# Stacking queries and keys by transfers inside the SBUF instead of by 0/1 matmuls, in a gated cross-attention and mixture-of-experts block

## The reference, cut to what matters

```python
# x (16, 256, 256), ctx (16, 256, 256): 16 batches, 256 tokens, 256 features; 16 heads of 16 dims
q = proj(layernorm(x), w_q, b_q); k = proj(ctx, w_k, b_k); v = proj(ctx, w_v, b_v)
scores = einsum('bhqd,bhkd->bhqk', q, k) / sqrt(16)
x = x + tanh(g_xattn) * (softmax(scores) @ v heads joined @ w_o.T + b_o)
# then: 8 experts of 256 -> 1024 -> 256, each token goes to its two best by sigmoid confidence * wealth
x = x + tanh(g_ffn) * sum over the two of weight * down(silu(gate(y)) * up(y)),  y = layernorm(x)
```

## Time and profile before

| | |
|---|---|
| median of 3 runs | 1134.77 us (1130.64 to 1135.57) |
| span of the profiled execution | 1132.2 us |
| TensorE busy | 1064.4 us, 94% of the span |
| VectorE, ScalarE, GpSimd busy | 57%, 48%, 33% |
| attention stage | up to about 445 us |
| one batch of the loop | 24.87 us |

### The profile page before, as it was taken

How to read it: one execution, slowest core, us unless ns; L and a number is a source line. 1 busy time by engine, 2 the same in 40 slices (tenths; PEclk the granted TensorE clock), 3 DMA queues, 4 the chain that set the end, 5 groups by cost and what they waited for, 6 DMA issues and landing times.

```text
span 1132.2 us, 24433 instructions
## 1 busy us (share of the span) xinstructions
PE 1064.4 (94%) x8310; PEld 889.4 (79%) x8310; DVE 650.5 (57%) x1577; ACT 547.2 (48%) x877; POOL 370.9 (33%) x444
## 2 busy tenths in 40 slices
PE   5799999999999978799999999999999999999994
PEld 4566677777777755475999999999679999999993
DVE  3657777877777764357444444444754444454442
ACT  4467777777777744346323333333643332333331
POOL 1223555555545542513212212212322121221221
PEclk8899999999999999999999999999999999999997
DMA  8010111111111173466312112112561121211211
GB/s 243 26 30 21 41 41 52 54 39 39 48 39 39 52 272 147 145 250 204 88 19 38 34 24 38 31 26 38 166 233 25 33 38 19 38 34 24 39 27 23
DMA packets 48698, 79.69 MB, mean 70 GB/s; under 512 B 6416, under 2 KB 42512, under 8 KB 44816
## 3 DMA queue, kind: packets, MB, share of 16 engines
q0 software_dynamic: 18080, 50.93, 16.7%
q1 hardware_dynamic: 30576, 28.23, 8.6%
HBM read 53.69 MB, written 25.18 MB: 70 GB/s over the span
## 4 chain that ended last, share of the span: by engine, by line
PE 82%; ACT 6%; DVE 3%; issue 3%; POOL 3%; DMA 2%; SPq 1%; POOLq 0%; ACTq 0%; DVEq 0%
PE up L1456 16%; PE gate L1456 16%; PE down L1468 10%; PE down L1470 5%; PE pv L583 4%; PE scores L572 4%; PE scores L533 3%; PE misc L479 3%; PE maxps L547 2%; PE gate L1502 2%; PE down L1521 2%; PE up L1502 2%; PE misc L506 2%; PE misc L515 2%; ACT probs L764 2%
## 5 line engine op out<-in xcount | busy, mean ns | idle before, releaser
L1853 POOL DMA_INDIRECT out<-y,token x64 | 101.2, 1581 | 450.3 <-DVE y L1724 351.7
L1617 ACT ACTIVATE silu<-gate 128x512 f32<-128x512 f32 x128 | 76.7, 600 | 277.3 <-PE up L1456 277.3
L1715 DVE TENSOR_TENSOR h<-silu,up 128x512 f32<-128x512 f32 x128 | 88.0, 688 | 179.4 <-ACT silu L1617 179.4
L977 DVE TENSOR_REDUCE max_neg<-maxps 128x4 f32<-128x1024 f32 x128 | 156.5, 1222 | 58.7 <-PE maxps L547 58.7
L1468 PE MATMUL down<-w_split,h_hi 128*128 128x512 f32 x512 | 185.8, 398 | 0.0
L1456 PE MATMUL gate<-x_hi,w_split 128*128 128x256 f32 x1024 | 184.4, 282 | 0.0
L1456 PE MATMUL up<-x_hi,w_split 128*128 128x256 f32 x1024 | 183.7, 281 | 0.0
L764 ACT ACTIVATE probs<-scores 128x1024 f32<-128x1024 f32 x124 | 127.3, 1027 | 78.7 <-PE scores L572 77.7
L1456 PEld LDWEIGHTS gate<-x_hi,w_split 128*128 128x128 f32 x1024 | 148.8, 188 | 3.0
L1456 PEld LDWEIGHTS up<-x_hi,w_split 128*128 128x128 f32 x1024 | 147.9, 188 | 0.0
L1470 PE MATMUL down<-w_split,h_lo 128*128 128x256 f32 x512 | 144.1, 282 | 0.0
(11 more groups left out here) (206 smaller groups left out, 1799.2 us busy)
## 6 DMA issues: line engine op xcount, KB each, us to landing
xg<-dispatched SPq DMA_DIRECT2D x40, 272.0 KB, 2.9
stage<-gate_T POOLq DMA_DIRECT2D x10, 1024.0 KB, 7.7
stage<-up_T POOLq DMA_DIRECT2D x10, 1024.0 KB, 9.8
stage<-down_T POOLq DMA_DIRECT2D x10, 1024.0 KB, 11.8
ctxT<-ctxT SPq DMA_DIRECT2D x17, 256.0 KB, 2.9
x_all<-x SPq DMA_DIRECT2D x16, 256.0 KB, 5.2
out<-x_all SPq DMA_DIRECT2D x16, 256.0 KB, 2.1
out<-y,token POOLq DMA_INDIRECT x70, 3.8
```

The source lines that it names most:

```text
L977: V.tensor_reduce(to, maxps[:], AX.X, ALU.max, negate=True).then_inc(s["max_taken"], 1)
L1617: nc.scalar.activation(silu[pair % 2][:], gate[pair % 2][:], ACT.Silu).then_inc(s_silu, 1)
L1715: V.tensor_tensor(h[pair % 2][:], silu[pair % 2][:], up[pair % 2][:], ALU.mult).then_inc(s_made, 1)
L1853: pool.indirect_dma_start(out, bass.IndirectOffsetOnAxis(token[:, t:t + 1], axis=0), y[:, t, :], None, compute_op=ALU.add).then_inc(s_adde ...
```

## The change

Batches 0 and 1 are stacked by matmuls as before. From batch 2 on SyncE stacks: after the last unit of scores of batch b is written it issues three transfers from the split keys of batch b+2 to every fourth partition of `keys`, and three for the queries. For that the three terms of a dimension lie on neighbouring partitions (`STEP` = 4 rows a dimension, three of them terms, the fourth zero or SHIFT, which is now the last row of each half), and the columns of the projections are ordered so that a transfer's source runs over all 128 partitions and its destination over 32. `max_scores` contracts over 63 rows instead of 48. The 0/1 matrices take whole 128-row blocks (twice the data to load and to convert) and live in `ctx_high` and `ctx_rest` until these are needed. In ScalarE's body `read_q` moves ahead of `exps(b, 6)`. `split` now waits for the transfers of the batch before instead of a unit.

```diff
-        UNITS = ["S0", "S1", "S2", "S3", "S4", "K0", "S5", "S6", "S7", "K1", "Q0", "Q1"]
+        UNITS = [f"S{pair}" for pair in range(HPAIRS)]
+        FIRST_PAIRS = [*range(0, HPAIRS, HC), *range(1, HPAIRS, HC)]
+        STACKED = 16 * TERMS
...
-            load(((probs[0][:, :, 0, :], pick_rows),), "picks_loaded")
+            load(((probs[0][:], pick_rows),), "picks_loaded")
...
+            def stack(b, what, to):
+                sp.wait_ge(s["q_split" if what == "Q" else "k_split"], b + 1)
+                parts = (high, rest, high) if what == "Q" else (high, high, rest)
+                for term, part in enumerate(parts):
+                    sp.dma_start(to[term::STEP].bitcast(fp32), part[what][:].bitcast(fp32)).then_inc(
+                        s["q_stacked" if what == "Q" else "k_stacked"], 16)
...
                 if back:
                     store_residual(b - 1, use)
+                if ahead:
+                    sp.wait_ge(s["unit_written"], unit(b, f"S{HPAIRS - 1}") + 1)
+                    stack(b + 2, "K", k[par])
+                    stack(b + 2, "Q", q[par])
                 if nxt:
                     store_shift(b + 1, 1 - par, use)
...
-                for i in range(QT):
-                    for part, source in (("high", high), ("rest", rest)):
-                        for half in range(HPP):
-                            r = slice(half * STACK, (half + 1) * STACK)
-                            last = mm(scores[:, half * QT + i, :], picks[f"{what} {part}"][r, i, :], source[what][r, c, :],
-                                      start=part == "high", stop=part == "rest")
+                for i in range(BLOCKS):
+                    for m, source in enumerate((high, rest)):
+                        picks = picks_of(what)[m]
+                        last = mm(scores[:, i, :], picks[:, i * P:(i + 1) * P], source[what][:, c, :], start=m == 0, stop=m == 1)
...
+                elif nth == 0:
+                    pe.wait_ge(s["k_stacked"], b * STACKED - STACKED)
+                    pe.wait_ge(s["q_stacked"], b * STACKED - STACKED)
...
-                stack_ahead("K0")
                 weigh(b, par, 1)
...
-                stack_ahead("K1")
...
-                stack_ahead("Q0")
                 weigh(b, par, 3)
-                stack_ahead("Q1")
...
                 read_pv(b, 1)
-                exps(b, 6)
                 if ahead:
                     read_q(b + 2, use)
+                exps(b, 6)
                 exps(b, 7)
...
-            def split(b, what, use, units):
+            def split(b, what, use):
                 use.read(alone, what)
-                if not is_first(b):
-                    alone.wait_ge(s["unit_written"], units)
+                if isinstance(b, int) and b == 2:
+                    alone.wait_ge(s["unit_written"], 2 * len(STACKS))
+                else:
+                    alone.wait_ge(s["q_stacked" if what == "Q" else "k_stacked"], b * STACKED - 2 * STACKED)
```

More of the change, by code:

```diff
@@ L154, in attention_stage @@
         rest = {what: sb(f"{what}_rest", [P, HC, SEQ], f32r) for what in "QK"}
-        picks = {what: sb(f"picks_{what}", [P, QT, P], f32r) for what in ("Q high", "Q rest", "K high", "K rest")}
         q = [sb(f"queries{i}", [P, HPAIRS, SEQ], f32r) for i in range(2)]
@@ L275, in read, with picks_of @@
                 eng.wait_ge(misc_read[n], uses + 1)
-        UNITS = ["S0", "S1", "S2", "S3", "S4", "K0", "S5", "S6", "S7", "K1", "Q0", "Q1"]
+        def picks_of(what):
+            held = (c_high[0], c_high[1]) if what == "Q" else (c_rest[0], c_rest[1])
+            return [part[:].rearrange("p c s -> p (c s)") for part in held]
+        UNITS = [f"S{pair}" for pair in range(HPAIRS)]
         STACKS = ["K0", "Q0", "K1", "Q1"]
+        FIRST_PAIRS = [*range(0, HPAIRS, HC), *range(1, HPAIRS, HC)]
+        STACKED = 16 * TERMS
         def units_before(b):
-            last = isinstance(b, int) and b == BATCHES - 1
-            return b * len(UNITS) + (2 * len(STACKS) if not last else len(STACKS))
+            return b * len(UNITS) + 2 * len(STACKS)
         def unit(b, what):
-            order = [n for n in UNITS if n not in STACKS] if isinstance(b, int) and b >= BATCHES - 2 else UNITS
-            return units_before(b) + order.index(what)
+            return units_before(b) + UNITS.index(what)
         def is_last(b):
@@ L860, in body @@
             def body(b, par, use, ahead, nxt, back, late):
-                def stack_ahead(what):
-                    if ahead:
-                        read_stack(par, what[0], int(what[1]), unit(b, what))
                 exps(b, 0)
@@ L971, in read_v, with maxima @@
                 last.then_inc(use.freed("V"), 1)
-            def maxima(b, pair):
-                dve.wait_ge(s["max_scored"], b * HPAIRS + (pair + 1))
+            def maxima(b, nth, order=range(HPAIRS)):
+                pair = order[nth]
+                dve.wait_ge(s["max_scored"], b * HPAIRS + (nth + 1))
                 to = max_neg[:].rearrange("p t (u n) -> p u t n", u=HPP)[:, :, :, pair]
@@ L1065, in vector_attention @@
             for n, what in enumerate("QK"):
-                for m, part in enumerate(("high", "rest")):
-                    last = V.tensor_copy(picks[f"{what} {part}"][:], probs[0][:, 2 * n + m, 0, :].rearrange("p (i c) -> p i c", i=QT))
+                for m in range(2):
+                    last = V.tensor_copy(picks_of(what)[m], probs[0][:, 2 * n + m].rearrange("p t s -> p (t s)"))
             last.then_inc(s["picks_ready"], 1)
@@ L1080, in vector_attention @@
             for pair in range(3):
-                maxima(0, pair)
+                maxima(0, pair, FIRST_PAIRS)
             rest_part(1, "K")
@@ L1086, in vector_attention @@
             read_v(0, PRO1)
-            maxima(0, 3)
-            maxima(0, 4)
+            maxima(0, 3, FIRST_PAIRS)
+            maxima(0, 4, FIRST_PAIRS)
             rest_part(1, "Q")
             for pair in range(5, HPAIRS):
-                maxima(0, pair)
+                maxima(0, pair, FIRST_PAIRS)
                 if pair < 7:
@@ L1232, in body @@
                     scale_x(b + 2)
-                    split(b + 2, "K", use, units_before(b) + (UNITS.index("K1") + 1 - len(UNITS)))
+                    split(b + 2, "K", use)
                 if isinstance(b, int) and b == 1:
@@ L1238, in body @@
                 if ahead:
-                    split(b + 2, "Q", use, units_before(b) + (UNITS.index("Q1") + 1 - len(UNITS)))
+                    split(b + 2, "Q", use)
                 if late:
@@ L1256, in gpsimd_attention @@
             return scatter_next_to_last, scatter_last
-        handed = dict(over=attention_over, s=s, units=units_before(BATCHES - 1) + sum(n not in STACKS for n in UNITS))
+        handed = dict(over=attention_over, s=s, units=units_before(BATCHES - 1) + len(UNITS))
         return sync_attention, tensor_attention, scalar_attention, vector_attention, gpsimd_attention, handed
```

49 lines of the change are left out of this document (22 added, 27 removed).

## The result

The changed kernel takes 1174.44 us (median of four runs, 1173.02 to 1177.57) against 1134.9 on the same chip: ratio 1.0343, 95% interval 1.0315 to 1.0371. It is slower, as forecast, but by 3.4% where 1.7% was forecast. The profiled execution has this span, against the 1132.2 of the earlier trace rows.

What follows compares the result with a forecast made beforehand. Bound: the loop from score 0 through the maxima's turn to the shift's landing. Thirteen steps of +0.7 and +0.55 make +16, with start and first two batches +19: span 1151, median 1154 us; forecast case 1143 to 1170, 8-in-10 range 1130 to 1192.

Steps and rivals of the forecast that it cites:

- the copy of Q: ScalarE's read_q ahead of exponentials 6: score 7 starts 0.78 us later, the turn of the maxima 0.8 later.
- The rule on which it rested: Loop from score 0 to the shift: even with free transfers a batch stays at 24.87 us, by -0.2 to +0.3.
- slow copies: Rival: SBUF-to-SBUF stacking transfers at half rate, 187 to 215 GB/s, +2.8 to +3.9 us a batch, 1174 to 1211; chance 0.2.
- not held up: Rival: stacking transfers finish before the shift's and the clock holds, -0.2 to +0.3 us a batch, 1134 to 1142; chance 0.18.
- faster: Rival: before the turn, removing K0 gains its full 0.7 us; -0.9 a batch, 1126 in total; chance 0.12.
- The thirteen steps: Score 0 to next score 0, batches 1 to 14: each +0.7 us of wait and +0.55 of clock, together +16.
- a middle: Shift's bytes, queued behind the six transfers, move between 271.35 and 273.0; 272.1 taken, score 0 at 272.9, +0.7 us a batch.
- one batch in three: TensorE idle before score 0: the clock dips in one batch in three, 1.7 us each, +0.55 a batch.
- the upper end: Clock term's range of 0 to 1.7 us a batch: at its top every batch pays for the dip.
- K0 and K1: Stacking matmuls removed before the turn: K0 gains 0 to 0.1 us, K1 nothing before the turn.
- The start: Before score 0 of batch 0: larger 0/1 matrices, longer conversions and more stacking units, 2 to 5 us, +4 taken.
- The next two steps: Batches 0 and 1 have more between turn and score 0 and lose less: -1 us against the rule.

Runs made afterwards that it cites:

- e1: Changed kernel without its six stacking transfers a batch, so later batches compute other values; 1138.5 us, ratio 1.0036.
- e9: Changed kernel with GpSimd's four scatters issued behind the context split and the bias addition; 1139.3 us, ratio 1.0030.
- e4: Changed kernel with 20 needless matmuls between the projection of V and score 0 of each batch from 2 on; 1158.4 us, ratio 1.0193.
- e15: e14 with GpSimd's addition of the bias moved from behind the context split to before the split of Q; 1151.5 us, ratio 1.0127.
- e13: Kernel before the change with only the copy of Q (read_q) moved ahead of exponentials 6; 1143.9 us, ratio 1.0067.
- e14: e11 with VectorE's statistics of the batch after next moved behind the first reduce of the maxima; 1148.5 us, ratio 1.0108.
- e18: Changed kernel, copy of Q put back, GpSimd's context split and bias ahead of Q's split, scatters held until the shift has landed; 1154.6 us, ratio 1.0168.
- e2: Changed kernel with the same six transfers at a quarter of the bytes each, so it computes other values; 1139.7 us, ratio 1.0021.
- e11: Changed kernel with the scatters late and the copy of Q put back behind exponentials 6; 1148.7 us, ratio 1.0108.
- e10: Changed kernel with the shift issued from ScalarE's queue and the next context's load held until the residual is stored; 1162.7 us, ratio 1.0223.
- e19: As e18, but with the copy of Q left ahead of exponentials 6, where the change put it; 1167.1 us, ratio 1.0275.
- e8: Changed kernel with a third buffer of stacked keys, K's three transfers issued earlier, right behind K's split; 1144.6 us, ratio 1.0074.

## Why the prediction was right or wrong

**Right.** The direction and the mechanism. The kernel is bounded by the loop from score 0 over the maxima to the shift, the stacking's TensorE time turns into waiting, score 7 waits behind the copy of Q, and the shift is held up by bytes on the DMA engines. The rule on which it rested, that a batch wouldn't get shorter even with free transfers, holds: e1 has 25.31 us against 24.87. Of the rivals the slow copies are out by the rate, 354 GB/s in the changed kernel and 383 in e9, with both ends in the SBUF; not held up and faster fall with the wait of 5.8. By its time alone, 1174, the result would have looked like the slow copies (1174 to 1211); only the profile tells the two apart.

**Two terms failed, and the larger is the bytes ahead of the shift.** The thirteen steps were to add 16 us and added 38. Per batch, by the medians, the wait is 5.8 instead of 4.5 (+1.3), the low clock takes 1.4 instead of 0.55 (+0.9), and the stretch at full clock gives back 0.4.

**The wait.** The prediction gave 271.35 to 273.0 for when the shift's bytes could move and took 272.1, a middle. On its own scale (turn at 268.40) the engines were through 4.6 us after the turn, at 273.0: its latest. The shift landed 0.9 behind that. It had all parts: 1.57 MB and half of the 1.2 MB that other transfers move. What was wrong is the choice of a middle between "the scatters come after" and "the scatters come before" where the timeline of before decides it: they are issued right behind the split of Q, so all but the last ahead of the shift. Its wait was 4.5 us, as long as before, behind a later turn; it measured 5.8. e9 moves the scatters' bytes away, and 1.6 us of wait go with them. The delay of the shift's issue by SyncE's queue, 0.36, is within the 0.45 that was allowed.

**The clock.** It was priced at one batch in three, +0.55. It is every batch, +1.4 each by e4; e4's whole gain, 16 us, stands against the 7 of the prediction. But the price was for an idle time of 1.6 us in front of score 0, and that became 2.64. e15 has the idle time of the prediction. The score 0 of two neighbouring batches, with the idle time in front of it, and the windows behind them:

```profile
255.82 0.50 PE L593 MATMUL scores<-queries,keys 64*128 64x256 f32 x4 [1.68 <-DMA queries<-max_rows]
281.98 0.50 PE L593 MATMUL scores<-queries,keys 64*128 64x256 f32 x4 [1.59 <-DMA queries<-max_rows]
```

```profile
256.20:259.70 3.50, 3.50 (x26) 2.81 (x24) 2.51 (x7) 1.98 (x2) 1.53 (x3) 0.65 0.50 162
282.40:285.90 3.50, 3.50 (x33) 3.00 (x32) 2.58 (x7) 2.05 (x2) 1.62 (x3) 1.00 0.48 177
```

In the ten batches from 5 to 14 of e15 the clock falls behind score 0 in four. So one in three was fair for the wait that the prediction expected; it wasn't worked out for the prediction's own latest landing, which leaves 2.5 us idle (273.8 less 271.3). The rows were there: after a stretch with TensorE 0.89 busy of 3.50 the clock fell, and the stretch before score 0 became 0.03 busy of 2.60. That every batch could pay stood as the upper end, and it was the case.

The two failures are one chain: the scatters make the wait long enough for the clock to fall, so they cost 35 of the 39.5 us, some 16 of them through the clock.

**The copy of Q** was priced at 0.8; alone in the kernel before it is 0.73 (e13). In the changed kernel the stretch at full clock is 20.71, 0.36 above before, since K0 and K1 did give something: 20.71 against e13's mean of 21.1, some 0.4 a batch where 0 to 0.1 was said. That part of the forecast was off in the other direction and hid some of the miss.

**The start** is +2.55 in this execution where +4 was said. One profile doesn't price it: over the 17 kernels with the change score 0 of batch 0 comes between 44.28 (e14) and 50.68 (e18), with a median of 47.7, and in the three without it between 43.9 and 44.7. By that the start costs some 3.2 us, near the forecast. The four conversions take 1.4 us instead of 0.9, less than the 0.8 more that was said. The next two steps give +0.6 instead of -1. (The prediction's own terms, 1 + 0.8 + 5 x 0.4 to 0.8, give 3.8 to 5.8 and not the 2 to 5 that it states.) Of the 2.4 us behind score 0 of batch 15, 0.9 are lost in the first 11 us, in whose first 10 us the granted clock is 0.53 against 0.66 before; the rest wasn't looked into.

**Where the expected gain went.** 2.9 us of TensorE work a batch were removed. Nearly none came back as time, because little of it stood in the loop; and e1, e2 and e9 show the next limit 0.3 to 0.5 us above the kernel before: the copy of Q on ScalarE ahead of exps 6, 0.7 by e13, and in e1 VectorE, whose work from the turn on fills the time until it has to reduce. That no version here beats the kernel before is measured; that none can isn't shown. Not tried are e11 with the bias alone moved, and e11 with GpSimd's `split_ctx` and `add_bias` placed where VectorE runs reductions alone.

## What to carry to other kernels

Work that is moved from an engine to the DMA engines is paid in bytes at a place in time: list every transfer issued in the microseconds ahead of the one that somebody waits for, other engines' too, and count them all as ahead of it unless the trace shows otherwise; here the order of four scatters was worth 35 us. A wait of 2.6 us on TensorE in each period cost its length and then 1.4 more in clock, so when the length of a wait is uncertain, price the clock at both of its ends. When something is added to hold a second effect still, as the 20 matmuls were, first work out what floor it sets for the first. The same holds for an edit that is stacked on another: the statistics moved in e14 set a floor that hid what e15 was to show.

## What the runs showed of the hardware that was not expected

- Copies inside the SBUF, 256 KB in pieces of 2 KB, six at once: 354 to 383 GB/s with the engines full (the lower rate with scatters among them), about the rate of the loads from HBM of the earlier trace rows with 1 KB pieces (373).
- SyncE needs 0.60 to 0.65 us for the issue of each such transfer, one after the other, and the shift's two issues took 1.94 instead of 1.35.
- Two queues didn't separate two transfers: on a queue of its own the shift still took 3.36 us to land (e10), against 3.47 behind the six.
- The clock is not a matter of the idle time in front of score 0 alone: it held behind 1.21 us (e9), fell in four of ten batches behind 1.6 to 1.7 (e15), in ten of twelve behind 1.8 to 2.1 (e10) and in every one behind 2.2 to 2.9 (the changed kernel). In e19 nothing idles in front of score 0, and it falls elsewhere.
- VectorE's operations on 2 to 16 columns beside one of GpSimd's on 512 took 0.7 to 1.2 us instead of 0.15 to 0.18 and ended with it; reductions out of the PSUM (1.23) showed no such effect. Beside the scatters' issue most of them kept their 0.17; one in the changed kernel's batch above took 0.54 (at 263.45) and ended with that issue.
- At the jump back of a loop of six batches' code VectorE stood for 3.6 us (e8) and that batch took 5 us longer; the loop of the kernel before, two batches long, has all its periods from batch 4 to batch 14 within 0.02 us of each other.
